# Six weight sets in place of three in the sorted normalised experts, five in place of three in the sorted routed output

## What is computed

```python
for e in range(E):
    routed = routed + comb[:, e:e + 1] * (h_expert @ expert_out_weight[e].T)
return (out_shared + routed).reshape(Bx, Tx, Cx)
```

```python
h = jax.nn.relu(jnp.einsum('td,edh->teh', xf, W1) + b1[None])
y = jnp.einsum('teh,ehd->ted', h, W2) + b2[None]
mu = jnp.mean(y, axis=-1, keepdims=True)
var = jnp.mean((y - mu) ** 2, axis=-1, keepdims=True)
y = (y - mu) / jnp.sqrt(var + EPS) * gamma[None] + beta[None]
y_sel = jnp.take_along_axis(y, topi[:, :, None], axis=1)
```

## Time and profile before

| what | us |
|---|---|
| median of 3 runs | 3437.53 |
| lowest and highest | 3427.68, 3438.13 |
| the profiled execution | 3433.94 |
| its span in the trace | 3432.2 |

### The profile page before, as it was taken

One profiled execution on the slowest core, in us unless ns is written; L12 is line 12 of the kernel. 1 busy time (PEld: TensorE's weight loads), 2 busy tenths in 40 slices (PEclk: granted clock), 3 DMA queues, 4 the chain that ended last, 5 costly groups with the idle time before them and its releaser, 6 DMA issues. The chain is left out here.

```text
span 3432.2 us, 53128 instructions
## 1 busy us (share of the span) xinstructions
PE 2519.3 (73%) x18781; PEld 2109.8 (61%) x18781; DVE 1643.4 (48%) x3169; ACT 1102.1 (32%) x2154; POOL 522.7 (15%) x805
## 2 busy tenths in 40 slices
PE   6978698599676687549688888888888885433334
PEld 4867597599466356438567777777777774333323
DVE  3646322322366311334377777777777774333113
ACT  2333121122133111012155555555555552231100
POOL 0000122122121015000001111111111112002112
PEclk9999699699798799769899999999999997666655
DMA  4000122243310027216634114424444201202231
GB/s 114 1 7 1 55 86 86 68 134 98 90 65 25 25 101 250 49 35 247 245 97 109 58 35 115 117 63 108 130 115 131 77 23 38 50 1 96 89 98 64
DMA packets 145018, 291.44 MB, mean 85 GB/s; under 512 B 36146, under 2 KB 73048, under 8 KB 141684
## 3 DMA queue, kind: packets, MB, share of 16 engines
q1 hardware_dynamic: 124532, 231.40, 21.9%
q0 software_dynamic: 20224, 56.65, 6.1%
HBM read 496.49 MB, written 65.74 MB: 164 GB/s over the span
## 5 line engine op out<-in xcount | busy, mean ns | idle before, releaser
L2215 PE MATMUL tx_ring<-g_ident,tx_p 128*128 128x128 f32 x2552 | 427.3, 299 | 128.6 <-issue 45.4
L2215 PEld LDWEIGHTS tx_ring<-g_ident,tx_p 128*128 128x128 f32 x2552 | 315.5, 151 | 222.9 <-issue 63.6
L2434 DVE TENSOR_REDUCE tx_neg_max<-tx_scores 128x1 f32<-128x1354 f32 x232 | 362.2, 1561 | 28.1 <-PE tx_scores L2203 28.1
L2441 DVE COPY tx_p_t<-tx_ring 128x512 f32<-128x512 f32 x464 | 306.9, 687 | 135.5 <-PE tx_ring L2215 130.1
L2341 ACT ACTIVATE tx_p<-tx_scores,tx_neg_max 128x1354 f32<-128x1354 f32 x232 | 322.3, 1389 | 77.1 <-DVE tx_neg_max L2434 76.8
L2203 PE MATMUL tx_scores<-tx_keys,tx_queries 96*128 96x512 f32 (+1 forms) x696 | 222.4, 432 | 13.7 <-DMA tx_queries<-tx_q_hi 11.3
L2348 ACT ACTIVATE tx_p_t<-tx_ring 128x384 f32<-128x384 f32 x232 | 113.4, 489 | 357.8 <-PE tx_ring L2215 356.7
L2753 PE MATMUL nee_wide<-nee_xg_t,nee_w 128*128 128x128 f32 x232 | 55.3, 414 | 156.6 <-issue 156.6
L2254 PE MATMUL tx_ring<-tx_p_t,tx_values 128*32 128x128 f32 x5104 | 151.3, 274 | 21.2 <-ACT tx_p_t L2348 20.8
L2254 PEld LDWEIGHTS tx_ring<-tx_p_t,tx_values 128*32 128x32 f32 x5104 | 135.8, 110 | 34.7 <-ACT tx_p_t L2348 34.0
L2753 PEld LDWEIGHTS nee_wide<-nee_xg_t,nee_w 128*128 128x128 f32 x232 | 48.2, 308 | 165.3 <-issue 165.3
(11 more groups left out here) (907 smaller groups left out, 5430.6 us busy)
## 6 DMA issues: line engine op xcount, KB each, us to landing
tx_keys<-expert_keys SPq DMA_DIRECT2D x696, 169.5 KB
lv1e_w<-in_L_ffn_W SPq DMA_DIRECT2D x232, 256.0 KB
tx_w<-in_L_ffn_W SPq DMA_DIRECT2D x58, 1024.0 KB
lv0e_w<-in_L_ffn_W SPq DMA_DIRECT2D x200, 256.0 KB
tx_values<-expert_values SPq DMA_DIRECT2D x58, 704.0 KB
tx_rows<-in_L_ffn_rows SPq DMA_DIRECT2D x29, 640.0 KB, 3.7
g_adj_t<-in_adj_t POOLq DMA_DIRECT2D x4, 3872.0 KB, 23.1
sro_we<-_L_ffn_expert_out_weight SPq DMA_DIRECT2D x29, 512.0 KB
```

Of the source, the lines that this page charges most:

```text
L2215: last = nc.tensor.transpose(ring[u % 2][:, (t - t0) * P:(t - t0 + 1) * P], p[n % 2][:, t * P:(t + 1) * P], g.ident[:])
L2434: nc.vector.tensor_reduce(neg_max[:, n % 4:n % 4 + 1], sc[n % 2][:, 0:N], AX_X, ALU.max, negate=True)\
L2441: nc.vector.tensor_copy(p_t[:, n % TURNED, t0:t0 + nt, :], ring[u % 2][:, 0:nt * P].rearrange("p (t q) -> p t q", q=P))\
```

## The change

Two constants:

```diff
-ROUTED_SETS = 3
+ROUTED_SETS = 5
 ROWS_AHEAD = 8
@@
-SETS = 3
+SETS = 6
```

## The result

| what | us |
|---|---|
| before, median of 4 runs | 3435.57 (3427.68 to 3438.13) |
| with the change, median of 4 runs | 3254.80 (3253.88 to 3259.43) |
| ratio | 0.948, 95% interval 0.9461 to 0.9499 |
| the profiled execution with the change | 3259.43 |
| its span | 3257.7 |

Faster by 5.2%, some 181 us. The forecast was 3276 with a range of 3258 to 3305: right in sign and in the circle that the change cuts, wrong in what binds once it is cut, and 3 us outside the range, on the fast side.

What follows compares the result with a forecast made beforehand. Three sets held the normalised stage in a wait circle; DMA would bind next. 26 tiles at 3.7 us (96.2 for 255.7) gain 159.5, routed stage 0: 3433.9 to 3274.4, forecast 3276 us with the run median's offset, range 3258 to 3305.

Steps and rivals of the forecast that it cites:

- The circle: Normalised stage: weight load, product and earlier tile's output wait on each other, 11.52 us a turn; afterwards spread over four tiles, 2.9 each.
- The count of loads: Normalised stage: 26 real weight loads in place of 21, 3.9 MB more, their price within the 3.7 us a tile.
- Rival D: Normalised stage: each real load costs 11.5 us as a rate, not a delay; slower, about 3458 us; chance 0.03.
- rival E: Whole change: no gain, as SBUF or the waits leave the lead unused; 3437 us; chance 0.01.
- The DMA term: Normalised stage: DMA engines bind next, 1.05 MB a tile at 285 GB/s, 3.7 us a tile for 26 tiles.
- rival B: Normalised stage: SP's issue of loads binds at 3.2 us a tile, gain 172.5 us, 3263 us; chance 0.17.
- The clock: Normalised stage: PE's clock falls now and then, PE catches up at full clock, and the mean stays at the DMA's rate.
- rival A: Normalised stage: PE at half clock throughout, 4.5 us a tile, gain 138.7 us, 3297 us; chance 0.20.
- The last tiles: End of the normalised stage: tiles needing no load also taken at 3.7 us, within PE's 2.2 to 4.5 us.
- The routed stage: Five sets there, 28 real loads for 24: taken as 0 us, with -3 and +4 as bounds.

Runs made afterwards that it cites:

- the last series: Runs of the unaltered change beside variants with 128 KB more per load, three DMAs a load, or both; the change measured 3255.66 us.
- the half run alone: Three sets in the normalised stage and five in the routed one, against the kernel before: 3434.20 us, ratio 0.9997.
- the first normalised half: First run with six sets in the normalised stage and three in the routed one, against the kernel before: 3269.75 us, ratio 0.9522.

## Why the prediction was right or wrong

**The circle** was right. Output, issue, landing, product, output: with three sets one tile a turn, with more SETS - 2. Four sets came out at 5.53 us a tile that needs a load, and six sets ended SP's wait for outputs.

**The count of loads** was right: 26 for 21 by 20.49 MB in the stage. Their price stood in the time a tile: 3.40 us with a load, 2.48 without, an estimate of 4.6 us for the five. Rival D, a load as a rate of 11.5 us, and rival E fell with the first profile.

**The DMA term** failed: "I take 3.7 us, the DMA's figure, as the start of this very stage is its nearest row." It measured 3.40 (3.24 in the last series), and it wasn't the DMA engines that set it. The 285 GB/s of the earlier trace rows stood beside a DMA share of 0.85, so the engines had gaps in that row, and it was a lower bound and no rate. The row of the routed stage said 318 at 0.89, and I named it, but gave it only to rival B. B is what happened: SP's 3.18 us, read from the earlier trace rows, turned out as 3.20 with stretches of delay on top, in the mean 3.4. Twenty-three tiles by 0.3 us are 6.8 us.

**The clock** was right: "I expect it to fall now and then." Its mean was 0.97 in the bulk, with PE busy 38.96 of 58 us: it stood at 1.2 GHz from 3148 to 3151 us, again from 3209.5 to 3212.5 in the last tiles, and at 2.4 GHz between. The sum had no term for it and needed none. So rival A fell, and with it what the Trainium skill says (TensorE: Matmul & The Clock Gate, HAM oscillation) for bursts shorter than the DMA wait behind them: here the burst of some 2.2 us was in the main longer than the wait that followed (26.6 us in front of line 2753 for 29 tiles), and only a few bursts ran slow. The row of the routed stage at 1.00 was the better guide.

**The last tiles** failed too: 3.7 us for tiles that need no load. They took 2.48, since PE without a gap is the bound there, at a mean granted clock of 0.77, between the 2.21 and 4.18 us that the prediction had for the two levels: 3.7 us in the sum. From first(28) to the end of the last output it took 7.7 us for 9.05, another 1.4.

**The routed stage** at 0 was right within what can be measured, by the half run alone (0.9997).

Together, against the profiled execution: 6.8 + 3.7 + 1.4 us in the stage and 3.3 us by which first(2) started earlier, which is scatter of the stages ahead (the first load is issued at 3118.2, 3119.0 and 3120.7 us in three profiles of the change, before at 3121.1), make 15.2; between 3274.4 and 3259.4 it is 15.0. The median lies another 4.6 us under that execution, where I had added 1.6. And the range ended at 3258 since I put its lower end at rival B with 3.2 us for all tiles; that end had no room for last tiles shorter than any load, and none for the 12 us by which the level of this kernel moves from one series to another.

The Trainium skill's figure (DMA: Bandwidth & Descriptors, Specifications) of about 358 GB/s from HBM for a core was the better guide here than my row: the highest mean in any of these stretches is 357 GB/s. As a hard limit the trace doesn't bear it out, since single slices of 2.7 us in the first profile of the change moved up to 396 GB/s. As the prediction said of that estimate, rival B then holds.

## What to carry to other kernels

A buffer's depth is not its number of sets but the number less the tiles that lie between the load's release and its use; write the circle down once with its durations and divide. When a rate is taken from a row, look at the share beside it: the 285 GB/s at a share of 0.85 were a lower bound, and the next limit was the queue that issues, whose time per load went with the number of DMAs (2.59, 3.20 and 3.68 us for three, four and five) and not with their bytes. Where that queue binds, join small transfers to large ones.

## What the hardware showed that I had not expected

The DMA share and the rate don't go together. At a share of 0.97 the change moved 317 GB/s; the kernels with more bytes or fewer issues moved 345 to 357 at 1.01. A share close to one did not mean that nothing more could go through. The share counts the time of packets, and that is no fixed price: in the change of the last series SP's packets of 2 KB took 96 ns in the mean where 84 was the median, and with more bytes 91.

The same kernel had two levels, 3255 and 3267 us, in different series, while the kernel before stayed within some 3 us. The chip alone does not explain it: the series at 3267.41 and the one at 3255.66 are both recorded on chip 4. In the profile at 3267.41 a tile took 3.66 us (84.3 us from first(2) to first(25)) at 277 GB/s, and what differs there is SP. Its loads stood 3.79 us apart in the mean, for 3.32, though it waited for an output only once, for 0.5 us, and its steps were uneven. In the profiles of the lower level the issues of lines 2698, 2700 and 2702 are 0.63 and 0.61 us apart and 0.33 us long. Here:

```profile
3166.76 0.02 SPq L2698 DMA_DIRECT2D nee_w<-in_L_ffn_w  x1
3167.51 0.02 SPq L2700 DMA_DIRECT2D nee_w<-in_L_ffn_w  x1
3167.57 0.33 SPq L2702 DMA_DIRECT2D nee_b<-in_L_ffn_cols  x1
```

SP's register moves, which wait for nothing, are uneven too. Of those ahead of its DMAs (3118 to 3215 us) 31 to 49% came over 30 ns off their usual 71 ns in the four profiles of the series at 3267. In the series of the first normalised half (3269.75) it was 26% there, 10% with four sets and 33% with five. In the profiles of the change and its variants in the other series, and in that of the kernel before, it was 2% or less. So the upper level goes with an uneven SP, and a kernel that SP's issues bind would show it where one that waits in a circle doesn't. What makes SP uneven is not shown.
